# A one-element GpSimd multiplication ahead of each indirect transfer, each waiting for the last one's semaphore

## What is computed

```python
# layer 0: every token takes 2 of 8 experts, and a shared network
shared = silu(xf @ w1) * (xf @ w3) @ w2
s = sigmoid(concat([xf, tf]) @ router_W)
_, topk_idx = top_k(s + router_bias, 2)
gates = s_sel / (s_sel.sum() + 1e-9)
h = gelu(einsum('nc,ech->enh', xf, W1e)); y = einsum('enh,ehc->enc', h, W2e)
x = x + (shared + einsum('ne,enc->nc', combine, y)) / 3
# layer 1: h starts as cond, z runs over the 256 steps of x
gate = sigmoid(h @ Wh.T + z_t @ Wz.T + b)
h = tanh(h * (1 - alpha) + gate * z_t)
x = x + hs
```

## Time and profile before

| | |
|---|---|
| runs, us | 1001.31, 1001.55, 998.25 |
| profiled execution: span from first to last instruction | 1155.6 us (its whole time is not given apart from this) |
| PE / PEld / DVE / ACT / POOL busy | 79% / 55% / 62% / 45% / 24% of the span |
| mean granted TensorE clock | 0.879 of full speed |
| GpSimd instructions that the profile counts | 318 |
| transfers issued by GpSimd (q0, software) | 13856 packets, 39.86 MB |
| one section in the profiled execution | some 133 us |

### The profile page before, as it was taken

One profiled execution on the slowest core, in us unless ns is written; L12 is line 12 of the kernel. 1 busy time (PEld: TensorE's weight loads), 2 busy tenths in 40 slices (PEclk: granted clock), 3 DMA queues, 4 the chain that ended last, 5 costly groups with the idle time before them and its releaser, 6 DMA issues.

```text
span 1155.6 us, 29134 instructions
## 1 busy us (share of the span) xinstructions
PE 910.9 (79%) x9550; PEld 633.8 (55%) x9550; DVE 716.7 (62%) x2491; ACT 516.3 (45%) x1431; POOL 275.5 (24%) x318
## 2 busy tenths in 40 slices
PE   2178769976999589986899779995999859998653
PEld 2067338843687247852588336862578426874432
DVE  5246447855777287754778457773878547657754
ACT  3155226632475145732466225742467324653333
POOL 1500730056002530045100550035300560005000
PEclk7599979987999789987999879996899879999955
DMA  7782323332243222532233322532223322322010
GB/s 239 246 256 78 124 73 93 112 108 75 72 130 124 88 66 72 142 100 78 81 102 103 115 69 65 145 114 83 73 66 111 107 77 75 106 88 74 10 29 19
DMA packets 91746, 115.24 MB, mean 100 GB/s; under 512 B 10930, under 2 KB 81108, under 8 KB 91604
## 3 DMA queue, kind: packets, MB, share of 16 engines
q1 hardware_dynamic: 77028, 73.43, 22.0%
q0 software_dynamic: 13856, 39.86, 10.7%
q10 hardware_dynamic: 720, 0.05, 0.1%
HBM read 56.68 MB, written 56.62 MB: 98 GB/s over the span
## 4 chain that ended last, share of the span: by engine, by line
PE 40%; DVE 16%; another core or an unknown queue 16%; ACT 10%; issue 10%; DMA 5%; POOL 2%; SPq 1%; DVEq 0%; ACTq 0%; POOLq 0%
PE bank L1127 36%; DVE pre L974 3%; PE bank L1250 3%; DVE hid_low L919 3%; DMA x_pair<-x_slots_even 3%; DMA x_pair<-x_slots_odd 2%; POOL x_slots_even L547 1%; DVE prod L906 1%; DVE zr L961 1%; ACT hid_high L674 1%; SPq L427 1%; ACT th L685 1%; DVE hs_low L981 1%; ACT hist L696 1%
## 5 line engine op out<-in xcount | busy, mean ns | idle before, releaser
L974 DVE TENSOR_TENSOR_SCAN pre<-th,zr 128x128 f32<-128x128 f32 x256 | 108.3, 423 | 232.2 <-ACT th L685 220.1
L1127 PE MATMUL bank<-hs_high,gwt_high 128*128 128x32 f16 x1024 | 81.2, 181 | 119.6 <-ACT hs_high L695 96.9
L685 ACT ACTIVATE th<-bank 128x64 f32<-128x64 f32 x256 | 59.5, 232 | 255.2 <-remote 164.6
L529 POOL TENSOR_TENSOR fence_pool<-zeros 128x1 f32<-128x1 f32 x48 | 12.3, 256 | 673.4 <-DVE is_low L869 353.5
L1127 PE MATMUL bank<-xe_high,w1e_high 128*128 128x128 f16 x768 | 161.3, 227 | 5.2 <-DVE xe_low L892 2.7
L1127 PEld LDWEIGHTS bank<-hs_high,gwt_high 128*128 128x128 f16 x1024 | 65.9, 100 | 171.7 <-ACT hs_high L695 125.7
L1127 PE MATMUL bank<-xe_low,w1e_high 128*128 128x128 f16 x768 | 159.3, 221 | 0.9 <-issue 0.9
L1127 PE MATMUL bank<-xe_high,w1e_low 128*128 128x128 f16 x768 | 158.9, 220 | 0.2
L695 ACT ACTIVATE hs_high<-pre 128x64 f16<-128x64 f32 x256 | 66.5, 260 | 188.0 <-DVE pre L974 176.8
L1127 PE MATMUL bank<-xs_high,w_high 128*128 128x512 f16 x256 | 109.6, 428 | 20.4 <-DVE prod L906 19.9
L1127 PE MATMUL bank<-xs_low,w_high 128*128 128x512 f16 x256 | 110.3, 431 | 2.8 <-issue 2.8
(11 more groups left out here) (162 smaller groups left out, 2307.4 us busy)
## 6 DMA issues: line engine op xcount, KB each, us to landing
x_pair<-x_slots_even SPq DMA_DIRECT2D x48, 256.0 KB
y_slots_even<-y_pair SPq DMA_DIRECT2D x48, 256.0 KB
x_pair<-x_slots_odd SPq DMA_DIRECT2D x48, 256.0 KB
y_slots_odd<-y_pair SPq DMA_DIRECT2D x48, 256.0 KB
x_tok<-in_x_dram SPq DMA_DIRECT2D x32, 256.0 KB, 5.3
out_dram<-o_tok SPq DMA_DIRECT2D x128, 64.0 KB, 1.7
x_slots_even<-zeros POOLq DMA_DIRECT2D x1, 3072.0 KB, 14.9
x_slots_odd<-zeros POOLq DMA_DIRECT2D x1, 3072.0 KB, 12.5
```

What stands on the lines that cost most here:

```text
L529: nc.gpsimd.tensor_tensor(fence_pool[:], zeros[:, 0:1], zeros[:, 1:2], ALU.mult).then_inc(s_fence, 1)
L685: nc.scalar.activation(flat3(th[:, s % 2, :, :, 1]), gate_sums(s), ACT.Tanh, scale=0.5 / UP).then_inc(s_th, 1)
L974: dve.tensor_tensor_scan(every(pre[:, s % 2]), every(th[:, s % 2]), every(zr[:, s % 2]), 0.0, ALU.mult, ALU.add).then_inc(s_pre, 1)
L1127: return pe.matmul(out_ap, w, mov, start=start, stop=stop, skip_group_check=True)
```

## The change

A second semaphore `s_issue` and a second one-element tile `fence_issue` are added. `pass_issue(count)` waits until `s_issue` has reached `count`, which is the number of such multiplications issued so far, and then issues one more, which adds one. It stands ahead of every one of the 256 indirect transfers; one more multiplication, without a wait, stands at the start. The fences stay. In the loop the count depends on the section, so it is worked out in a register.

```diff
+            MOVES = TOPK * NJ
+
+            def pass_issue(count):
+
+                pool.wait_ge(s_issue, count)
+                nc.gpsimd.tensor_tensor(fence_issue[:], zeros[:, 0:1], zeros[:, 1:2], ALU.mult).then_inc(s_issue, 1)
+
+            def scatter_tiles(par, tiles, before):
+
                 for j in tiles:
                     for k in range(TOPK):
+                        pass_issue(before + (j - tiles[0]) * TOPK + k)
                         pool.indirect_dma_start(x_slots[par], at_slots(x_slots, par, j, k), x_tok[:, par, j, :], None
                                                 ).then_inc(s_scat, 16)
 
-            def gather(b, j):
+            def gather(b, j, before):
                 par = b.n % 2
                 for k in range(TOPK):
+                    pass_issue(before + k)
                     pool.indirect_dma_start(y_got[:, j % NYG, k, :], None, y_slots[par], at_slots(y_slots, par, j, k)
                                             ).then_inc(s_got[j % NYG], 16)
...
             nc.gpsimd.tensor_tensor(fence_pool[:], zeros[:, 0:1], zeros[:, 1:2], ALU.mult).then_inc(s_fence, 1)
-            scatter_tiles(0, range(NJ))
+            nc.gpsimd.tensor_tensor(fence_issue[:], zeros[:, 0:1], zeros[:, 1:2], ALU.mult).then_inc(s_issue, 1)
+            scatter_tiles(0, range(NJ), 1)
```

More of the change, by code:

```diff
@@ L149, in moe_gated_recurrence @@
         fence_pool = sb("fence_pool", [P, 1])
+        fence_issue = sb("fence_issue", [P, 1])
         mask = sb("mask", [P, NJ, E])
@@ L274, in moe_gated_recurrence @@
         s_fence = sem("s_fence")
+        s_issue = sem("s_issue")
         s_och = sem("s_och")
@@ L541, in scatter @@
                 pass_fence(b.g * FENCES + 1)
-                scatter_tiles(par, range(0, SCAT_FIRST))
-            def scatter_tiles(par, tiles):
+                scatter_tiles(par, range(0, SCAT_FIRST), 1 + MOVES + b.g * (2 * MOVES))
+            MOVES = TOPK * NJ
[3 more added lines that the diff above has]
+            def scatter_tiles(par, tiles, before):
                 for j in tiles:
                     for k in range(TOPK):
+                        pass_issue(before + (j - tiles[0]) * TOPK + k)
                         pool.indirect_dma_start(x_slots[par], at_slots(x_slots, par, j, k), x_tok[:, par, j, :], None
                                                 ).then_inc(s_scat, 16)
-            def gather(b, j):
+            def gather(b, j, before):
                 par = b.n % 2
                 for k in range(TOPK):
+                    pass_issue(before + k)
                     pool.indirect_dma_start(y_got[:, j % NYG, k, :], None, y_slots[par], at_slots(y_slots, par, j, k)
@@ L566, in body @@
                     pass_fence(b.g * FENCES + 2)
+                    issued = 1 + MOVES + b.g * (2 * MOVES) + (TOPK * SCAT_FIRST if b.prep else 0)
                     for j in range(NYG):
-                        gather(b, j)
+                        gather(b, j, issued + TOPK * j)
                     if b.prep:
-                        scatter_tiles((b.n + 1) % 2, range(SCAT_FIRST, NJ))
+                        scatter_tiles((b.n + 1) % 2, range(SCAT_FIRST, NJ), issued + TOPK * NYG)
+                        issued = issued + TOPK * (NJ - SCAT_FIRST)
                     for j in range(NYG, NJ):
```

## The result

The changed kernel takes 1005.32 us (median of four runs, 1004.72 to 1006.35) against 1000.43 of the kernel before (four runs, 998.25 to 1001.55). The ratio is 1.0057 with a 95% interval from 1.0040 to 1.0074: 4.9 us slower (4.0 to 7.4 by the interval), which is just over the 0.5% taken as the border of what can be told. 1006 had been forecast.

The account below looks back on a forecast made before the run. No engine was taken as the limit; what counts is where someone awaits GpSimd's transfers. The start's 2.9 us plus section 0's 2.0 us made 4.9 us on 1001.3, forecast 1006 us, range 1000 to 1020.

Parts of the forecast that it names:

- One multiplication: Between two GpSimd transfers, an added multiplication costs its length less 0.12 us; 0.17 us taken, 0.08 to 0.59 possible.
- The wait on the semaphore without a price: Ahead of each new multiplication, the wait costs nothing, since the earlier multiplication was done before the transfer between them started.
- the register operation in the loop: Working out the count in the loop costs nothing, done by the sequencer while the previous transfer takes 0.97 us.
- The start: Sixteen multiplications in the scatter chain before PE's first transpose, plus one without a wait: 2.9 us, paid in full.
- Section 0: Gathers awaited by DVE, 18 multiplications ahead of group 3 exposed: 3.1 us, of which 2.0 counted; from 0 to 6.7.
- Sections 1 to 7: Added multiplications in the later bodies are hidden, by the recurrence steps in sections 1 to 6: nothing paid.
- The room left in section 2: Slack before DVE takes section 2's gathers: 3.1 us at group 0, 4.2 at group 3; 1.1 us to spare.
- The halts: PE's halts during indirect transfers, 159 us of remote waits, belong to the profiled execution; some 5 us at most in runs.
- the faster rival: Transfers further apart lessen the PE halts left in a run: 10 us gained gives 996 us; chance 0.07.
- the profiled execution was to grow by 2.9 us: The profiled span grows by the start's cost alone, to 1158 or 1159 us, if the halts stay as they are.

Follow-up runs that it names:

- chip 9: One of two chips of the follow-up runs; there the unedited changed kernel took 1119.0 us, ratio 0.9657 to the kernel before (1154.5 us).
- the halting chips: Chips 9 and 12, where all twelve follow-up experiments ran; the unedited kernel before took 1154 to 1159 us at the median there.

## Why the prediction was right, and where it was not

**The time.** 4.9 us were summed, 4.9 measured, in an interval from 4.0 to 7.4. It is a sum of two terms that each have an answer in the trace, but it is closer than its parts, and that closeness is luck.

**One multiplication.** Taken at 0.17 us, in a range from 0.08 to 0.59. The 256 of the changed kernel last 0.262 on average, which makes 0.14. The wait on the semaphore without a price, as argued from the fences: shown by the kernel without it. The price at the start is 0.09 for most (0.39 less 0.30). No run shows a price for the register operation in the loop either: on chip 9 the changed kernel's median pitch is 1.38 us both at the start, where there is none, and in the bodies.

**The start.** 2.9 us forecast. From profile to profile it is 3.2 (56.52 less 53.35). That is partly luck: over the eight profiles without multiplications there the first transpose lies between 53.35 and 55.54 us, 54.4 on average, and over four with one of a column each it is 55.43 to 56.64, 56.3 on average. So 1.9 us is the better number, and the term was 1.0 us too large.

**Section 0.** Exposed, as forecast, for the reason forecast: GpSimd is late itself, DVE waits. 2.0 us were counted of a possible 3.1. DVE's wait is 5.4 us in the changed kernel and 2.1 in the kernel before on chip 9, but these two do not subtract: 2.2 of the 5.4 stand at group 3, which the kernel before takes behind a halt of 13.0 us. The cleaner number is GpSimd's own. From the first scatter ahead of these gathers to the end of the eighth gather it takes 23.9 and 24.2 us in the two profiles of the kernel before and 26.35 in the changed kernel, 2.2 to 2.5 us more for 18 multiplications. So 2.0 is near, by a price for each that was too high (0.17 against 0.12 to 0.14) and a part of it taken off by estimate. The two terms together come to some 4.1 to 4.4 us. That DVE's wait comes back in the run's time one for one was not shown apart.

**Sections 1 to 7.** Hidden, as forecast: no wait of `r_part` in the changed profile. The room left in section 2, forecast as 1.1 us at the tightest, is 2.8 to 3.4 there: group 0 is issued by 346.17 and, with landing as in section 0 some 1.8 us behind, is there at 348.0, DVE takes it at 351.28. By the same reckoning it is 2 us or more in every other section but section 6, where group 1, issued by 793.95 and taken at 796.91, has 1.2. With three multiplications it is gone.

**The halts.** Here a step failed. The sentence was "I conclude that these halts belong to the profiled execution and are nearly absent in the runs". By their times they were absent in the runs with which the change was compared, so taking them out was right for those and gave rooms of the right size. But the reason was wrong: profiled executions without them exist (span 1002.7 for a run of 1004.7), and ordinary runs with them too (1157 us). I had matched 159 us of waits to 154 us of difference and took the only difference I knew of, profiled or not, for the cause; a difference between the places of run and profile fits the same sum. The match was also closer than it deserved, since PE's 52.7 us of longer busy time at the lower clock stood beside the waits and was not in the sum. What the mistake costs is the sign on the halting chips: the faster rival was given 0.07 and some 10 us at most, where the change gains 35. And where halts stay, the profiled execution was to grow by 2.9 us; on chip 9 it went from 1152.4 to 1113.8.

What causes the halts is only in part settled. They need indirect transfers in quick succession. ACT's `th` has 149 us of remote waits with transfers 1.27 us apart, 110 and 142 at 1.38, 13 at 1.53 and none at 1.60. The distance is not all of it: in section 0, 1.38 us is enough, and in the later sections it is not. A look at one in the kernel before, on chip 9, and the load of the DMA engines from 391 to 399 us in 40 slices, in tenths:

```profile
391.87 0.27 PE L1127 MATMUL bank<-hs_low,gwt_high 128*128 128x32 f16 x4
...
398.94 0.23 ACT L685 ACTIVATE th<-bank 128x64 f32<-128x64 f32 x1 [7.39 <-remote]
...
DMA  2006844003664000975000686200890000395000
```

PE's last matmuls of the step start at 391.87, and ACT, which needs only their semaphore, starts 7.1 us later. The DMA engines stand idle between any two transfers, so no backlog of data shows there. Whether PE finishes late or its signal arrives late can't be told, since the ends of matmuls are modelled in the profile. Signals in general are not late: ACT's `hs_high` starts within 0.20 us of the end of DVE's `pre` in all 256 steps, in the kernel before as in the changed one. Why the same kernel shows this in one place and not in another stays open, and no experiment tells the chip from its neighbours' load, the placement of the data or the hour.

## What to carry to other kernels

A small instruction between two long ones of the same engine costs its length less what the engine would have waited for anyway, and that only where somebody awaits the engine: find those places in the chain and in the waits, take out what an unusual execution hides, and sum those alone. Keep it short: over one element it did not lengthen DVE's instructions here, over 80 columns it did. When a profiled execution is much longer than the runs beside it, time the same kernel again on the chip of the profile before you call it the profiler's doing. On a kernel whose GpSimd issues indirect transfers back to back while PE has short dependent steps, try some more distance between them, and stop where their consumer begins to wait.

## What the runs showed that was not expected

With indirect transfers 1.27 us apart, ACT gets PE's results up to 10 us late on two chips (kernel before 1156 us), and by its time not in the runs of 1000 us. A second one-element multiplication straight behind the first adds 0.15 us to the distance of two transfers and brought 91 us. A multiplication over 80 columns takes 0.36 us undisturbed and 0.408 on average, over one column 0.20 and 0.262; beside the former DVE's `zr` lasts 271 ns instead of 247.
